# Tokens turned from their centred form, convolution output added among the experts, tap products paired by GpSimd

## What is computed

```
xn   = groupnorm(x)
conv = deformable 3x3 convolution of xn, 8 groups of 4 channels: for each
       pixel and group, 9 points with learned offsets, bilinear samples,
       softmax-weighted sum, then @ w_out + b_out
tok  = x + conv                        # 256 tokens of 32 channels per image
ln   = (tok - mean) / std              # over the channels
att  = softmax(ln @ ln.T) @ ln         # per image
tok2 = tok + att
ln2  = (tok2 - mean) / std
p    = softmax(ln2 @ router_w + router_b); best two of 8 experts
out  = tok2 + sum over the two of gate * (ln2 @ expert_w + expert_b)
```

## Time and profile before

| what | value |
|---|---|
| median of 3 executions | 88.04 us (87.92 to 88.28) |
| the profiled execution's own time | 87.82 us |
| its span, first to last instruction | 86.1 us |
| busy share: TensorE, VectorE, GpSimd, ScalarE | 88%, 66%, 60%, 42% |
| granted TensorE clock, mean of the span | 0.89 |
| bytes read from and written to HBM | 0.81 MB, 0.26 MB |

### The profile page before, as it was taken

How to read it: one execution, slowest core, us unless ns; L and a number is a source line. 1 busy time by engine, 2 the same in 40 slices (tenths; PEclk the granted TensorE clock), 3 DMA queues, 4 the chain that set the end, 5 groups by cost and what they waited for, 6 DMA issues and landing times.

```text
span 86.1 us, 1669 instructions
## 1 busy us (share of the span) xinstructions
PE 76.1 (88%) x627; PEld 63.0 (73%) x627; DVE 57.0 (66%) x109; ACT 36.1 (42%) x91; POOL 52.0 (60%) x88
## 2 busy tenths in 40 slices
PE   1999999899999998997999999999894699989930
PEld 1889599789999967996999997669452398546400
DVE  1145400527995999999989967076327859999930
ACT  0442203796786349610000003559824611099800
POOL 5108999998896999999999750003304400147910
PEclk9999999999999999999999999999999555555555
DMA  0411441018900000000000000000000000000023
GB/s 0 125 37 27 109 65 14 9 30 258 252 12 0 4 8 0 0 4 0 0 0 11 0 0 0 0 8 0 0 0 0 0 8 0 0 0 0 0 52 70
DMA packets 5258, 2.37 MB, mean 28 GB/s; under 512 B 4433, under 2 KB 4786, under 8 KB 5250
## 3 DMA queue, kind: packets, MB, share of 16 engines
q1 hardware_dynamic: 4545, 2.00, 9.7%
q10 hardware_dynamic: 704, 0.26, 1.3%
HBM read 0.81 MB, written 0.26 MB: 12 GB/s over the span
## 4 chain that ended last, share of the span: by engine, by line
PE 35%; DVE 23%; issue 3%; ACT 2%; DVEq 0%
PE ps L645 10%; DVE prod L308 6%; DVE image_all L1084 6%; PE ps L632 4%; PE ps L732 3%; PE ps L802 3%; PE ps L789 3%; PE ps L751 2%; PE ps L832 1%; PE ps L767 1%; PE ps L714 1%; PE ps L674 1%; DVE tok_c L1251 1%; DVE prod L1247 1%; PE ps L698 1%
## 5 line engine op out<-in xcount | busy, mean ns | idle before, releaser
L544 PE MATMUL ps<-wide_ident 128*128 128x128 f32 x86 | 12.4, 299 | 1.8 <-POOL wide_ident L391 1.8
L1084 DVE TENSOR_TENSOR image_all<-ps,images 128x896 f32<-128x896 f32 (+4 forms) x8 | 13.2, 1689 | 0.4 <-PE ps L632 0.4
L544 PEld LDWEIGHTS ps<-wide_ident 128*128 128x128 f32 x86 | 11.2, 208 | 2.8 <-POOL wide_ident L391 1.8
L645 PE MATMUL ps<-wide_ident,image_all 128*128 128x128 f32 (+2 forms) x100 | 11.7, 274 | 0.9 <-DVE image_all L1084 0.9
L645 PEld LDWEIGHTS ps<-wide_ident,image_all 128*128 128x128 f32 (+2 forms) x100 | 10.9, 139 | 1.2 <-DVE image_all L1084 1.2
L632 PE MATMUL ps<-wide_ident,prod 128*128 128x128 f32 x81 | 9.9, 275 | 0.2
L632 PEld LDWEIGHTS ps<-wide_ident,prod 128*128 128x128 f32 x81 | 8.8, 141 | 0.8 <-DVE prod L308 0.7
L304 POOL TENSOR_TENSOR my<-prob,hat 128x384 f32<-128x384 f32 x8 | 7.9, 1008 | 0.7 <-DVE ps L304 0.7
L308 POOL TENSOR_TENSOR prod<-my,hat 128x1152 f32<-128x1152 f32 x3 | 8.0, 2650 | 0.2
L308 DVE TENSOR_TENSOR prod<-ps,hat 128x1152 f32<-128x1152 f32 x6 | 7.9, 1350 | 0.1
L929 ACT ACTIVATE sampT<-ps 128x128 f32<-128x128 f32 x2 | 0.8, 398 | 15.5 <-PE ps L698 15.5
(11 more groups left out here) (195 smaller groups left out, 147.7 us busy)
## 6 DMA issues: line engine op xcount, KB each, us to landing
images<-images SPq DMA_DIRECT2D x2, 300.0 KB, 4.1
images<-images SPq DMA_DIRECT2D x2, 280.0 KB, 3.6
x_tok<-in_x SPq DMA_DIRECT2D x4, 64.0 KB, 2.3
x_rows<-in_x SPq DMA_DIRECT2D x1, 128.0 KB, 3.1
x_rows<-in_x ACTq DMA_DIRECT2D x1, 128.0 KB, 3.4
expert<-in_expert_w SPq DMA_DIRECT2D x4, 32.0 KB
out_dram<-prod SPq DMA_DIRECT2D x2, 64.0 KB, 2.3
out_dram<-prod ACTq DMA_DIRECT2D x2, 64.0 KB, 2.5
```

Source lines behind the costliest of these rows:

```text
L544: pe.matmul(pbank(bank, P), ident, ident, start=True, stop=True)
L645: ins = pe.matmul(ps[0:last, SAMPLED, c * NJ:(c + 1) * NJ], taps[:, ty % SLOTS, tx, c, 0:last], ident, start=(ty == 0 and tx == 0 and c == 0),
L1084: v.tensor_tensor(taps[:, ty % SLOTS, t0:t1, :, y0 * NI:y1 * NI], bcast(coef_rows(ty, t0, t1).rearrange("p (t j) -> p t j", j=P)[:, :, y0 ...
```

## The change

It does six things, each in the diff below, which leaves out only the declarations of semaphores (conv_out, tok_ready become tok_turned, tokT_kept; taps_paired and x_mean_ready are new).

- The products of the square's row 3 (PAIRED) are added in pairs by GpSimd, taps 0 and 1, and taps 2 and 3; TensorE turns tap 4 and row 4 first, then the two sums.
- ScalarE makes the mean of x (16 copies with a sum) and x_ctok (16 additions of a bias) in place of GpSimd.
- The centred tokens with tokens first come from turning the centred tokens with channels first, which VectorE copies out of PSUM (tok_cT); `tokens_first` and the additions and centring behind it go. GpSimd's tok is now x less 1, without the convolution.
- w_out times the samples is added to the output's banks PV (`add_conv`) among the experts, behind each residual.
- The first half is turned back to tokens ahead of the second half's weighted sums, and the first tokens are turned ahead of the second half's attention; ATT_OUT's first bank is another.
- Three `keep_warm` matmuls stand around the second tokens' turn, and the second half's bias goes ahead of the last product.

```diff
@@ -59,7 +59,8 @@
 OUT_OF_RACE = -1e30

 WARM = {"start": 5, "group sums": 5, "squares": 4, "normalised": 1, "hats": 22, "layer norm": 5,
-        "projection weights": 1}
+        "projection weights": 1,
+        "second token norm": 2}


 def bcast(ap, dim, n):
@@ -170,7 +171,6 @@
-        tok_s = sb("tok_s", [P, NT])
@@ -178,6 +178,7 @@
+        x_mean_tok = sb("x_mean_tok", [P, NT])
@@ -191,6 +192,7 @@
         def late_part(i):
             return late[:, i * NT * C:(i + 1) * NT * C]

+        tok_cT = late_part(8).rearrange("p (a t) -> p a t", a=GA)
         sqT = late_part(1).rearrange("p (a t) -> p a t", a=GA)
         rT = late_part(7).rearrange("p (a t) -> p a t", a=GA)
         tok2 = late_part(0).rearrange("p (t c) -> p t c", c=C)
@@ -263,11 +265,12 @@
         COEF = (0, 2)
         MY = (4, 5)
         SAMPLED, SPARE = 6, 7
+        PAIRED = 3
         SAMP_T = (7, 1, 2, 3)
         TOK_T, VAR_T = (5, 0), (4, 1)
-        CONV_OUT, PV = 2, 6
+        TOK_TURNED, PV = 3, 6
         SCORE = (4, 5, 6, 7, 0, 1, 2, 3)
-        ATT_OUT = (0, 1)
+        ATT_OUT = (5, 1)
         LN_BACK = (4, 5)
         EXPERT = (5, 3, 4, 1, 0, 3, 4, 2)
         EXPERT_ORDER = (0, 1, 2, 3, 4, 7, 5, 6)
@@ -505,21 +508,16 @@
             then(g.tensor_tensor(gen_x[:, 0, :], gen_x[:, 0, :], gen_x[:, 1, :], ALU.add))
             g.tensor_tensor(den[:, :], gen_x[:, 0, :], prob[:, 8, :], ALU.add).then_inc(den_ready, 1)

-            g.wait_ge(x_tok_ready, 1)
-            then(g.tensor_tensor(tok_q[:, :, 0:C // 2], xt[:, :, 0:C // 2], xt[:, :, C // 2:C], ALU.add))
-            for n in (8, 4, 2, 1):
-                then(g.tensor_tensor(tok_q[:, :, 0:n], tok_q[:, :, 0:n], tok_q[:, :, n:2 * n], ALU.add))
-            then(g.tensor_scalar(tok_q[:, :, 0:1], tok_q[:, :, 0:1], 1.0 / C, None, ALU.mult))
+            g.wait_ge(taps_ready, pieces_ready(PAIRED, len(PIECES[PAIRED]) - 1))
+            last = NI * pixels_of(PAIRED)[1]
+            for tx in (0, 2):
+                pair = taps[:, PAIRED % SLOTS, tx, :, 0:last]
+                g.tensor_tensor(pair, pair, taps[:, PAIRED % SLOTS, tx + 1, :, 0:last], ALU.add).then_inc(taps_paired, 1)
+
             for ga in range(GA):
                 t = slice(ga * GT, (ga + 1) * GT)
-                g.tensor_tensor(x_ctok[:, t, :].rearrange("p (h n) c -> p n h c", h=HALVES), x_tok[:, ga, :, :, :],
-                                tok_q[:, t, 0:1].to_broadcast([P, GT, C]).rearrange("p (n h) c -> p n h c", h=HALVES),
-                                ALU.subtract).then_inc(x_ctok_ready, 1)
-
-            for ga in range(GA):
-                t = slice(ga * GT, (ga + 1) * GT)
-                g.wait_ge(tok_centred, ga + 1)
-                g.tensor_scalar(tok[:, t, :], tok[:, t, :], -1.0, None, ALU.add).then_inc(tok_less_ready, 1)
+                g.tensor_scalar(tok[:, t, :].rearrange("p (h n) c -> p n h c", h=HALVES), x_tok[:, ga, :, :, :], -1.0, None,
+                                ALU.add).then_inc(tok_less_ready, 1)
             for ga in range(GA):
                 t = slice(ga * GT, (ga + 1) * GT)
                 g.wait_ge(att_ready, ga + 1)
@@ -635,17 +633,21 @@
                             first[tx // 4] = False
                 ins.then_inc(coef_done, 1)

-            def add_taps(ty):
+            def add_taps(ty, numbers, end=False):
+
+                last = NI * pixels_of(ty)[1]
+                for tx in numbers:
+                    for c in range(GC):
+                        ins = pe.matmul(ps[0:last, SAMPLED, c * NJ:(c + 1) * NJ], taps[:, ty % SLOTS, tx, c, 0:last], ident,
+                                        start=(ty == 0 and tx == 0 and c == 0), stop=(end and tx == numbers[-1]),
+                                        is_transpose=True, skip_group_check=True)
+                return ins
+
+            def add_row(ty):

                 for piece, (t0, t1) in enumerate(PIECES[ty]):
                     pe.wait_ge(taps_ready, pieces_ready(ty, piece))
-                    for tx in range(t0, t1):
-                        for c in range(GC):
-                            last = NI * pixels_of(ty)[1]
-                            ins = pe.matmul(ps[0:last, SAMPLED, c * NJ:(c + 1) * NJ], taps[:, ty % SLOTS, tx, c, 0:last], ident,
-                                            start=(ty == 0 and tx == 0 and c == 0),
-                                            stop=(ty == TW - 1 and tx == TW - 1), is_transpose=True,
-                                            skip_group_check=True)
+                    ins = add_taps(ty, range(t0, t1))
                 ins.then_inc(taps_used, 1)

             pe.wait_ge(upper_ready, 1)
@@ -656,17 +658,22 @@
             keep_warm(SAMPLED, WARM["hats"])
             add_weights(0)
             add_weights(1)
-            add_taps(0)
+            add_row(0)
             add_weights(2)
             pe.wait_ge(over_ready, 1)
             pe.wait_ge(x_proj_ready, 1)
             pe.matmul(ps[0:1, SPARE, 0:1], over_all[:, :], ones[:, 0:1], start=True, stop=True).then_inc(flag_sum, 1)
-            add_taps(1)
+            add_row(1)
             add_weights(3)
             add_weights(4)
-            add_taps(2)
-            add_taps(3)
-            add_taps(4)
+            add_row(2)
+            pe.wait_ge(taps_ready, pieces_ready(PAIRED, len(PIECES[PAIRED]) - 1))
+            add_taps(PAIRED, (4,))
+            add_row(4)
+            for pair in range(2):
+                pe.wait_ge(taps_paired, pair + 1)
+                ins = add_taps(PAIRED, (2 * pair,), end=(pair == 1))
+            ins.then_inc(taps_used, 1)
             def centred_input(ga):

                 for h in range(HALVES):
@@ -705,15 +712,19 @@
             tokens_channels_first(1)
             variance(0)
             variance(1)
-
-            def tokens_first(ga):
+            for ga in range(GA):
+                pe.wait_ge(tokT_kept, ga + 1)
+                for h in range(HALVES):
+                    ins = pe.transpose(pbank(TOK_TURNED, P, (ga * HALVES + h) * P), tok_cT[:, ga, h * P:(h + 1) * P], ident)
+            ins.then_inc(tok_turned, 1)
+
+            def add_conv(ga):

                 for side in range(2):
-                    out_ps = ps[64 * side:64 * side + 64, CONV_OUT + ga, 0:GT * C].rearrange("p (h n c) -> p h n c", h=HALVES, n=GI)
+                    out_ps = ps[64 * side:64 * side + 64, PV + ga, 0:GT * C].rearrange("p (h n c) -> p h n c", h=HALVES, n=GI)
                     for n in range(GI):
-                        ins = pe.matmul(out_ps[:, :, n, :], sampT[:, ga * GI + n, :, :],
-                                        w_out_bd[:, 2 * side:2 * side + 2, :], start=True, stop=True)
-                ins.then_inc(conv_out, 1)
+                        pe.matmul(out_ps[:, :, n, :], sampT[:, ga * GI + n, :, :],
+                                  w_out_bd[:, 2 * side:2 * side + 2, :], start=False, stop=False, skip_group_check=True)

             def channels_first(bank, src, ga):

@@ -726,8 +737,8 @@

                 pe.wait_ge(lnT_ready, ga + 1)
                 for q in range(GI):
-                    if SCORE[ga * GI + q] >= CONV_OUT and ga == 1:
-                        pe.wait_ge(tok_ready, SCORE[ga * GI + q] - CONV_OUT + 1)
+                    if SCORE[ga * GI + q] == TOK_TURNED:
+                        pe.wait_ge(tok_centred, 1)
                     for h in range(HALVES):
                         ins = pe.matmul(pbank(SCORE[ga * GI + q], 2 * P, h * 2 * P), lnT[q * C:(q + 1) * C, ga, h, :],
                                         lnT[q * C:(q + 1) * C, ga, :, :], start=True, stop=True)
@@ -755,6 +766,7 @@
             def att_to_tokens(ga):

                 pe.wait_ge(first_attT_ready if ga == 0 else attT_ready, 1)
+                pe.wait_ge(values_ready, GA)
                 for h in range(HALVES):
                     ins = pe.matmul(pbank(ATT_OUT[ga], P + GI, h * (P + GI)), attT[:, ga, h * P:(h + 1) * P], ident_sums[:, :],
                                     start=True, stop=True)
@@ -803,35 +815,40 @@
                                     expert4[q * C:(q + 1) * C, :, :], start=True, stop=True)
                 ins.then_inc(experts_done, 1)

-            tokens_first(0)
             scores(0)
-            tokens_first(1)
             scores(1)
             values_back()
             weighted(0)
+            att_to_tokens(0)
             weighted(1)
-            att_to_tokens(0)
-            att_to_tokens(1)
             pe.wait_ge(tok2_centred, 1)
             channels_first(2, tok_c, 0).then_inc(ln2T_done, 1)
+            att_to_tokens(1)
             pe.wait_ge(late_ready, 5)
             router(0)
+            keep_warm(EXPERT[1], WARM["second token norm"])
             pe.wait_ge(tok2_centred, 2)
+            pe.wait_ge(ln2T_ready, 1)
             channels_first(2, tok_c, 1).then_inc(ln2T_done, 1)
+            keep_warm(EXPERT[1], 1)
             router(1)
-            for n in EXPERT_ORDER[:6]:
+            for n in EXPERT_ORDER[:3]:
```

(58 more changed lines are left out.)

16 lines of the change are left out of this document (8 added, 8 removed).

## The result

The changed kernel takes 84.69 us (median of 4, 84.20 to 84.76) against 87.98 beside it (87.53 to 88.28). The ratio is 0.963, 95% interval 0.959 to 0.967: 3.3 us less. The forecast was 84.6.

What follows compares the result with a forecast made beforehand. Bound: TensorE's turns to 51.6 us, then TensorE, VectorE and ScalarE in rounds, then VectorE choosing, scaling and summing. Clock held, 0.40 + 1.75 + 0.71 + 0.55 = 3.41 off 87.82 gives 84.41, median 84.6; range 83.9 to 85.3.

Steps and rivals of the forecast that it cites:

- Part 1: Taps before the samples: GpSimd adding pairs saves TensorE 8 of 60 turns; gain 0 to 0.5 us, taken as 0.4.
- the collision that I feared: Before the samples: GpSimd's two x less 1 passes, 49.3 to 51.0 us, run over VectorE's w_out_c and could cancel the gain.
- Part 2: Centring x moved to ScalarE, idle before 52.33 us: 33 operations, 6 us, ending by 46 us; cost nothing.
- Parts 3 and 4: Centred tokens turned once, attention reordered: VectorE starts the second half 1.77 us earlier, taken as 1.75, including 0.43 from the single turn.
- my 62.25: Forecast start, in us, of the second weighted sums, queued behind the first half's turn back to tokens; end forecast 63.35.
- Part 5: Three dummies around the second tokens' turn: cost nothing, 0.58 us at most; held clock worth 0.71 us.
- The 0.71: Gain in us from held clock: 0.25 in the second tokens' turn plus 0.46 in the second router.
- Part 6: w_out among the experts: hidden under VectorE's 5.3 us with clock held, not at 1.2 GHz; earlier last bias gains 0.55 us.
- the 0.55 for the bias: At the end: bias ahead of the last product lets VectorE's last addition start at 82.18 instead of 82.73 us.
- Rival 1: Clock falls just behind the second router and TensorE becomes the bound: 86.7 us, chance 0.12.
- rival 3: Clock falls already in the weighted sums, near 61 us, with turns not counting as TensorE activity: slower, 90.5 us, chance 0.07.
- the case that hung on the dummies: Clock falling just behind the second router, forecast as still faster than before: 86.7 us, chance 0.12.

Runs made afterwards that it cites:

- experiment 9: The changed kernel with the second half's bias behind the last product again, as before the change: 84.98 us.
- experiment 6: The changed kernel without the 32 w_out records among the experts, so the convolution is missing from the result: 85.87 us.
- experiment 1: The changed kernel without its three new dummies: 88.97 us, ratio 1.019; also the kernel before with those three dummies alone: 87.78 us, ratio 1.001.
- experiment 7: Four experts ahead of the first residual instead of three: changed kernel without dummies, 87.50, 87.59 and 85.70 us; with dummies and sum of squares first, median 85.5.

## Why the prediction was right, point by point

**Part 1**, pairs: 0.40 forecast, 0.46 in the trace, 0.43 by undoing them. The way to it was another, so the number is partly luck. I had VectorE hold the samples, behind a w_out_c hindered by GpSimd and ending at 50.88, with TensorE done at 50.85. In fact w_out_c took 0.30 and ended at 50.54, the collision that I feared did not come, and TensorE ended at 51.12. Of the 0.88 us of turns saved, some 0.4 went into its waits for VectorE's products of row 4, which I had left out.

**Part 2**, centring on ScalarE: no cost. The work ends at 44.1, 6.8 us before TensorE uses it.

**Parts 3 and 4**, one turn and the new order: 1.75 forecast, 1.53 in the trace, and 0.9 of it by undoing the order alone. The other 0.6, the single turn's, no run undoes; for it stand the scores in one row and the three exponentials without a gap. The 0.22 between: the second weighted sums start at 62.05, which is 0.2 later than my 62.25 less the 0.4 of part 1, behind the turn back of the first half. ScalarE was late next for the first weighted sums, which wait for its second exponential, as I had it; its third ended at 61.56 and held nothing.

**Part 5**, clock: right that it would hold past the second router, and that the dummies stand in nobody's way. The 0.71 came out as 0.51, since the second logits now wait for ScalarE's deviation, which waits for VectorE's sum of squares behind the first logits. I had named no wait there.

**Part 6**: the 0.55 for the bias is in the trace, since VectorE's wait of 0.56 before the last addition is gone; with 0.1 elsewhere it makes the 0.66. But the order that I credited was not needed: with the clock held, the bias is done in time in either place (experiment 9). That step of mine failed, and its number stood by luck. Where the clock is at 0.50 the new order has a price: the last product stands behind both biases, and ScalarE's copy and output issues behind it (experiment 6).

**Sum**: 3.41 forecast, 3.2 in the trace, 3.3 in the medians.

**The rivals** were weaker than the forecast. Rival 1, the clock falling behind the second router, was priced at 86.7; experiment 1 is just that case, and it takes 88.97. Two terms of its sum failed. For the six experts I took the 3.95 of six in a row, less 1.0 for three warm ones; split three and three they took 1.08 + 3.71 = 4.79, which is 1.8 more (the split alone costs 1.4 to 1.8, experiment 7). The two experts behind the gates, for which I took a third of that row, 1.3, took 2.02. Together that is 2.6, against 2.3 missed; the two biases, 2.07 us in the trace in place of 2.4, go the other way. So a slower outcome was near: three matmuls of 0.29 us away, and not, as in my rival 3, a clock that falls in the weighted sums. I had the sign of the case that hung on the dummies wrong. On rival 3: from 45 to 50 us TensorE did nothing but turns, busy 4.96 of 5 us, and the granted clock stayed at 1.00 in this kernel too. By the rule of the Trainium skill that rival 3 names (page "TensorE: Matmul & The Clock Gate", Part 4) it should not have; the trace differs.

## What to carry to other kernels

Where TensorE's clock falls in the profile before an end that is still full of TensorE work, price the tail at both clocks before anything is moved into it: three dummies made 4.3 us of difference to the same edit. Dummies alone gave a ratio of 1.001, the rest alone 1.019, both together 0.963: such edits are to be tried together, and what undoing one costs is not what it gives alone. Taking work from a TensorE that then stands idle can cost time: without w_out the kernel is 1.2 us slower. (With the experts packed better it is 0.8 slower by the medians, of which the trace explains little.) And two single profiles are to be lined up at an instruction that the edit does not move before their times are compared: here that alone made up to 0.65 us.

## What I had not expected

- The clock's fall is not the same in all executions of one kernel. With four experts first and no dummies two of them take 85.70 and 87.50 us, in the old order 85.70 and 91.24, while the change stays within 0.56 in four.
- Matmuls on 32 rows ran side by side when they lay on different quarters of the rows, and one behind another when they shared one: 16 records of experts 0 to 3 took 1.17 us at 2.4 GHz, 12 records of experts 3, 4 and 7 took 1.99.
- A VectorE operation with two inputs took 0.30 us beside a GpSimd pass with one tile as input, 0.50 beside one with two tiles, and 0.69 beside x_ctok before.
